# Head attention over all 128 rows, features turned by VectorE, gate logits behind the last expert, and every order written anew

## The chip, the cores and the metric

One Trainium2 chip, and of it one core: TensorE, VectorE (DVE in the rows), ScalarE (ACT), GpSimd (POOL) and SyncE, which issues most transfers. The time of a kernel is its device time in microseconds. Of the kernel before there are three runs.

## What is computed

The input x and the context are 32 batches of 256 tokens with 256 features, all fp32.

```
x = x + tanh(g_xattn) * performer(layernorm(x), ctx, ctx)      # 16 heads of 16, 64 random features, causal
    proj = (q * 256**-0.25) @ random_features                  # [16, 64]; the same for k
    q' = exp(proj_q) + 1e-4;  k' = exp(-|k|^2/2 + proj_k - max over ALL batches of -|k|^2/2) + 1e-4
    out[l] = sum_{j<=l} (q'[l] . k'[j]) v[j] / sum_{j<=l} (q'[l] . k'[j])
x = x + tanh(g_ffn) * ffn(layernorm(x))
    h  = rmsnorm(x);  q = h @ Wq + bq;  k, v = ((h @ Wdown + bdown) @ Wup + bup), per head
    att = softmax(einsum('bthd,btgd->bthg', q, k) / 4)         # over the 16 HEADS of one token
    y2 = x + (einsum('bthg,btgd->bthd', att, v) @ Wo + bo)
    h2 = rmsnorm(y2);  gate = softmax(h2 @ Wg + bg)            # 8 experts
    out = y2 + einsum('btd,edf,bte->btf', h2, We, gate)        # all experts for all tokens
```

## The kernel before

One batch is a matrix of 256 tokens, held as two halves of 128 rows (index t). Exact fp32 products are made out of three rounded ones (`three_passes`): high by high, high by low, low by high, so an operand X has parts `X_hi` (written by ScalarE) and `X_lo` (the rest, by VectorE).

Each batch goes through these stages, named by letters in the signals: q (normalize x, turn x and the context, half norms), r (features: `fk`, `fq`, and their exponentials `ek0..3`, `eq0..3`, to which GpSimd adds 1e-4 in `pk0..3`, `pq0..3`), p (key-query products X00, X01, X10, X11 for the first 128 keys and Y0, Y1 for the second; ScalarE moves X to `att`, VectorE multiplies Y by the causal mask, GpSimd masks the diagonal of X in m00..m11; `av0..av3` multiply by the values, `nt_t` turns the numerators, `den_`, `numerators_over` divide, `attended` adds x), g and f (second normalization, `qq`, `dn`, `kv0`, `kv1`), head attention (scores s, softmax, mix pv), o (output projection, `y2`, second norm, turn of h2), e (gate g and experts `mm00..mm13`, mm1n being the second token half; `gated` adds one expert times its gate to `z`).

Every engine runs a list that was written out by hand for the first batches and then one order, `slot(n)`, repeated for all n: in a slot each stage works on another batch (features on n+2, attention on n+1, head attention on n, output on n-1, experts on n-2 and n-3). There is no planner in the kernel; the order of the calls in `slot` and in the prologue is all that sets it. The eight PSUM banks are dealt out by name in the dictionary `BANK`; two steps with the same bank exclude each other, and the waits `pe.wait_ge(*at(step, batch))` see to it. `if b in (...)` around a wait means that for other batches another wait already covers it.

What the change touches:

- The context and the normalized x are turned by TensorE with the identity, four 128x128 turns each (`keys_turned`, `queries_turned`, L1893), then `k_hi`, `q_hi` are copied from PSUM by ScalarE and `k_low`, `q_low` are taken by VectorE. The half norms h2 are turned by TensorE too (`h_tr_`, L2070).
- Feature products: 4 row groups of 32 rows, 512 columns (`feature_products`, L1915); `norm_products`, L1924, adds the norms with two sets of weights.
- Head attention: q, k and v of a token group are turned by VectorE in 32x32 blocks (`q_turned` L1413, `k_turned` L1441, `v_turned` L1458). ScalarE spreads the queries of the two token halves into `q_bd` with zeros elsewhere (`q_apart`, L854). `head_scores` (L1966) and `head_mix` (L1974) are 128 products each of 32 rows and 32 columns of the array, 16 columns wide, made in four parts of 32 (`PARTS`); `weights_exp` and `ssum_` give the sum of the weights.
- The gate: `gate_products` (L1980, L1982), 8 small products with weights `wg` of 16 columns, in bank g; `gate_bias` adds them up.

Of the kernel before, what the change touches and what calls it, by code (L numbers as in the profile page):

```python
# [5 lines left out]
F32 = mybir.dt.float32  # L6
# [5 lines left out]
P = 128  # L12
# [15 lines left out]
CHUNK_BUFFERS = 8  # L28


BANK = dict(x000=3, x001=7, x010=5, x011=0, y00=6, y01=5, av0=2, x100=6, x101=5, x110=0, x111=1, y10=3, y11=2,
            av1=4, fq0=4, fq1=6, fq2=3, fq3=1, fk0=1, fk1=5, fk2=6, fk3=2, c=5, h=0, x=3, nd0=2, nd1=5, ht=7,
            dn=4, qq=7, kv0=2, kv1=3, s=7, pv=4, otr=0, o=7, h20=2, h21=1, g=2, mm00=0, mm01=0, mm02=4,
            mm03=3, mm10=6, mm11=1, mm12=3, mm13=6)
STAB_BANK = BANK["ht"]
# [45 lines left out]
def build(nc, x_d, ctx_d, gx_d, gf_d, rf_d, g1_d, wq_d, bq_d, wdn_d, bdn_d, wup_d, bup_d,  # L81
          wo_d, bo_d, g2_d, wg_d, bg_d, we_d, out_d):
    ctx = ExitStack()
    with ctx:
# [18 lines left out]
        sel_tok, off_tok = sb("sel_tok", [P, 2]), sb("off_tok", [P, 2])  # L103
        neg_half = sb("neg_half", [P, 4])

        f_hi, f_lo, w_h = sb("f_hi", [P, P], F32R), sb("f_lo", [P, P], F32R), sb("w_h", [P, C, P], F32R)
        sel_h = sb("sel_h", [P, C, 2])
# [5 lines left out]
        wg = sb("wg", [P, C, 2 * E], F32R)  # L113
        we_hi, we_lo = sb("we_hi", [P, C, E * D], F32R), sb("we_lo", [P, C, E * D], F32R)
# [17 lines left out]
        down = sb("down", [P, L], F32R)  # L132
# [8 lines left out]
        q_t, k_t, v_t = sb("q_t", [P, H, 32]), sb("k_t", [P, H, 32]), sb("v_t", [P, HD, 32])  # L141
        q_bd = sb("q_bd", [P, 32, T, H])
        s_max, s_sub, s_exp = sb("s_max", [P, 32]), sb("s_sub", [P, 32, H]), sb("s_exp", [P, 32, H])
        s_sum, s_tok, s_rec = sb("s_sum", [P, 32]), sb("s_tok", [P, T, H]), sb("s_rec", [P, T, H])
        p_bd, p_t = sb("p_bd", [P, 32, T, H]), sb("p_t", [P, 32, 32])

# [4 lines left out]
        o_tok, o_n = sb("o_tok", [P, HD, T, H]), sb("o_n", [P, T, D])  # L151
# [18 lines left out]
        xn = sb("xn", [P, T, D])  # L170
        q_hi, q_lo = sb("q_hi", [P, C, L], F32R), sb("q_lo", [P, C, L], F32R)
        k_hi, k_lo = sb("k_hi", [P, C, L], F32R), sb("k_lo", [P, C, L], F32R)
        h2 = sb("h2", [P, T, 4, 2 * H])
        h_t = sb("h_t", [P, L], F32R)
        v1 = sb("v1", [P, T, H, 32])
        qf, kf = [sb("qf0", [P, PAIRS, L])], [sb("kf0", [P, PAIRS, L])]
# [5 lines left out]
        qf.append(sb("qf1", [P, PAIRS, L]))  # L182
        kf.append(sb("kf1", [P, PAIRS, L]))
# [4 lines left out]

# [5 lines left out]
        gates_in, gammas_in = transfer("gates_in", 1, 2), transfer("gammas_in", 1, 2)  # L194
        wq_in, wo_in, wdn_in, wup_in = transfer("wq_in"), transfer("wo_in"), transfer("wdn_in", 1, 2), transfer("wup_in", 1, 2)
        bdn_in, bqkv_in, bo_in, bg_in = transfer("bdn_in", 1, 2), transfer("bqkv_in", 1, 2), transfer("bo_in"), transfer("bg_in")
        wg_in, we_in, rf_in = transfer("wg_in"), transfer("we_in", 1, 2), transfer("rf_in", 1, 8)

        w_pool = signal("w_pool", "zero_id one_tri ident tri f_scale f_hi f_lo")
        w_act, wa_high, wb_act = signal("w_act", "tanh"), signal("wa_high", "wq wdn wup wo"), signal("wb_act", "wg we0 we1 we2 we3")  # L200
        w_dve = signal("w_dve", "zero_f zero_v1 v1_one half sel_h w_h gamma2")
        wa_dve, wb_dve = signal("wa_dve", "wdn wq wup bkv wo"), signal("wb_dve", "wg we0 we1 we2 we3")
        w_tok = signal("w_tok", "sel_tok off_tok")
        ctx_act, ctx_dve = signal("ctx_act", "square"), signal("ctx_dve", "sum")
        stab_dve, stab_pe = signal("stab_dve", "most min col stab less0 kept less"), signal("stab_pe", "row all")

        batch_signals = [  # L210
            signal("q_pe", "h_tr"),
            signal("q_pe_b", "c_t x_t"),
            signal("q_dve", "h_lo"),
            signal("q_dve_b", "q_st q_mv q_bn k_lo q_lo"),
            signal("q_act", "h_hi"),
            signal("q_act_b", "h_t_"),
            signal("q_act_c", "xn q_hi"),
            signal("q_act_d", "k_hi"),
            signal("q_pool", "rstd q_r"),
            signal("r0_pe", "fk"),  # L220
            signal("r0_pe_b", "fq"),
            signal("r0_act", "ek3"),
            signal("r0_act_b", "ek1"),
            signal("r0_act_c", "ek0"),
            signal("r0_act_d", "ek2"),
            signal("r0_act_e", "eq0"),
            signal("r0_act_f", "eq3"),
            signal("r0_act_g", "eq1"),
            signal("r0_act_h", "eq2"),
            signal("r0_pool", "pq0"),  # L230
            signal("r0_pool_b", "pk0"),
            signal("r0_pool_c", "pk2"),
            signal("r0_pool_d", "pk3"),
            signal("r0_pool_e", "pk1"),
            signal("r0_pool_f", "pq2"),
            signal("r0_pool_g", "pq1"),
            signal("r0_pool_h", "pq3"),
            signal("p0_pe", "X00 X01 Y0 av0 av1"),
# [42 lines left out]
        def at(step, b):  # L281
            return signal_of[step].at(step, b)
# [2321 lines left out]
```

## Time and profile before

| | |
|---|---|
| median of 3 runs | 1260.78 us (1250.12 to 1265.76) |
| the profiled execution, span from its first to its last instruction | 1252.8 us |
| TensorE busy | 1193.6 us, 95% |
| TensorE weight loads (beside the products) | 978.2 us, 78% |
| VectorE busy | 942.0 us, 75% |
| ScalarE busy | 728.5 us, 58% |
| GpSimd busy | 568.1 us, 45% |
| mean granted TensorE clock | 0.988 |

The profile tells of one execution; its span lies 8 us under the median of the runs. Busy time is the union of an engine's instructions, so instructions that overlap count once. In a timeline the second number is the length of a group from its first start to its last end; neighbours overlap, since an instruction's last results are still on their way when the next has started. 40.20 MB are moved in all, 32 GB/s, most of it in the first 30 us, when the whole context is read for the maximum of the half norms.

### The profile page before, as it was taken

What the parts mean: (1) busy time and instruction counts of PE and PEld (TensorE: products, weight loads), DVE (VectorE), ACT (ScalarE), POOL (GpSimd) and SP (SyncE); (2) the same over time, 40 slices, a digit from 0 to 9 for tenths busy, and PEclk for the clock granted to TensorE, in tenths of its full rate; (3) what the DMA queues carried; (4) which work ended last, traced back from release to release, by engine and by line L of the source; (5) the groups of instructions that cost most, each with busy time, mean ns of one, the idle gap of its engine ahead of it and who ended that gap; (6) DMA issues with size and microseconds to landing.
All of it is one profiled execution on the core that took longest, in us unless ns stands there. A gap on an engine that the chain in (4) does not pass through costs nothing.

```text
span 1252.8 us, 55905 instructions
## 1 busy us (share of the span) xinstructions
PE 1193.6 (95%) x25347; PEld 978.2 (78%) x25347; DVE 942.0 (75%) x2206; ACT 728.5 (58%) x1467; POOL 568.1 (45%) x887
## 2 busy tenths in 40 slices
PE   1689899999999999999999999999999999999988
PEld 1467678888888888888888888888788888888876
DVE  7576567787777778777877777777787777777875
ACT  7577545566656556665655665565566656555430
POOL 3455515545444554544445454434545444554320
PEclk9988989999999999999999999999999999999999
DMA  9310000000000000000000000000000000000000
GB/s 304 96 36 20 20 10 29 20 29 28 28 12 28 28 20 28 29 28 11 28 28 20 28 29 28 13 26 29 20 29 28 29 12 28 29 19 11 12 20 17
DMA packets 39005, 40.20 MB, mean 32 GB/s; under 512 B 3440, under 2 KB 38512, under 8 KB 38768
## 3 DMA queue, kind: packets, MB, share of 16 engines
q1 hardware_dynamic: 38384, 36.59, 9.3%
q8 instruction: 199, 3.26, 1.1%
q14 instruction: 38, 0.31, 0.1%
q0 software_dynamic: 384, 0.04, 0.0%
HBM read 28.23 MB, written 8.39 MB: 29 GB/s over the span
## 4 chain that ended last, share of the span: by engine, by line
PE 93%; DVE 2%; DMA 1%; POOL 1%; issue 1%; ACT 1%; SPq 0%; DVEq 0%; POOLq 0%; ACTq 0%
PE ps L1899 14%; PE ps L1901 12%; PE ps L1900 12%; PE ps L1932 10%; PE ps L1947 7%; PE ps L1974 6%; PE ps L1966 6%; PE ps L1940 6%; PE ps L1893 4%; PE ps L1915 4%; PE ps L1957 2%; DMA c_chunk<-in_ctx 1%; PE ps L1982 1%; PE ps L2238 1%; PE ps L2336 1%
## 5 line engine op out<-in xcount | busy, mean ns | idle before, releaser
L1200 DVE SCALAR_TENSOR_TENSOR z<-ps,gate,z 128x256 f32<-128x256 f32 x512 | 245.4, 479 | 80.2 <-PE ps L1901 68.4
L1899 PE MATMUL ps<-we_hi,h_hi 128*128 128x512 f32 x512 | 215.6, 421 | 2.4 <-DVE z L1200 2.4
L1901 PE MATMUL ps<-we_hi,h_lo 128*128 128x512 f32 x512 | 203.9, 398 | 0.0
L1900 PE MATMUL ps<-we_lo,h_hi 128*128 128x512 f32 x512 | 203.7, 398 | 0.0
L1932 PE MATMUL ps<-qf,kf 64*128 64x256 f32 x1024 | 133.5, 401 | 5.1 <-POOL kf L474 2.1
L1899 PEld LDWEIGHTS ps<-we_hi,h_hi 128*128 128x128 f32 x512 | 97.4, 190 | 24.6 <-DVE z L1200 3.3
L453 POOL TENSOR_SCALAR z<-y,tanh_f 128x512 f32<-128x512 f32 x32 | 22.1, 692 | 205.5 <-DVE y L1433 205.3
L1932 PEld LDWEIGHTS ps<-qf,kf 64*128 64x128 f32 x1024 | 97.0, 193 | 23.5 <-issue 7.6
L1901 PEld LDWEIGHTS ps<-we_hi,h_lo 128*128 128x128 f32 x512 | 97.1, 190 | 23.0
L1900 PEld LDWEIGHTS ps<-we_lo,h_hi 128*128 128x128 f32 x512 | 97.5, 190 | 16.0
L1947 PE MATMUL ps<-att,v 128*32 128x256 f32 (+1 forms) x2048 | 98.5, 331 | 2.3 <-issue 1.4
L1966 PEld LDWEIGHTS ps<-k_t,q_bd 32*32 32x32 f32 x8192 | 76.2, 105 | 28.5 <-issue 27.8
L1974 PEld LDWEIGHTS ps<-v_t,p_t 32*32 32x32 f32 x8192 | 75.2, 104 | 21.4 <-issue 20.2
L1966 PE MATMUL ps<-k_t,q_bd 32*32 32x16 f32 x8192 | 83.2, 185 | 5.3 <-issue 5.2
L1947 PEld LDWEIGHTS ps<-att,v 128*32 128x32 f32 x2048 | 57.9, 110 | 36.4 <-issue 11.0
L1974 PE MATMUL ps<-v_t,p_t 32*32 32x16 f32 x8192 | 82.0, 184 | 1.4 <-DVE p_t L1221 0.9
L1940 PE MATMUL ps<-qf,kf 64*128 64x128 f32 x1024 | 76.8, 289 | 3.0 <-issue 1.5
L854 ACT ACTIVATE q_bd<-q_t,sel_tok 128x512 f32<-128x512 f32 x64 | 77.2, 1266 | 2.5 <-DVE q_t L1413 2.4
L1940 PEld LDWEIGHTS ps<-qf,kf 64*128 64x128 f32 x1024 | 64.8, 192 | 6.7 <-ACT att L713 2.5
L744 ACT ACTIVATE nt<-ps 128x512 f32<-128x512 f32 x32 | 19.1, 597 | 86.8 <-PE ps L1947 86.8
L525 POOL TENSOR_TENSOR y<-y,b_o 128x512 f32<-128x512 f32 x32 | 41.3, 1290 | 53.4 <-ACT y L917 53.4
L898 ACT ACTIVATE h_hi<-ps 128x256 fp32r<-128x256 f32 x32 | 12.4, 386 | 86.1 <-PE ps L2336 86.1
(217 smaller groups left out, 3056.1 us busy)
## 6 DMA issues: line engine op xcount, KB each, us to landing
c_in<-in_ctx SPq DMA_DIRECT2D x32, 256.0 KB, 4.0
x_in<-in_x SPq DMA_DIRECT2D x32, 256.0 KB, 2.8
out<-z SPq DMA_DIRECT2D x32, 256.0 KB, 2.2
c_chunk<-in_ctx SPq DMA_DIRECT2D x14, 512.0 KB, 8.8
stage<-in_L_ffn_We SPq DMA_DIRECT2D x2, 1024.0 KB, 9.3
c_chunk<-in_ctx SPq DMA_DIRECT2D x2, 256.0 KB, 8.2
stage_q<-in_L_ffn_Wq SPq DMA_DIRECT2D x1, 256.0 KB, 8.5
stage_u<-in_L_ffn_Wup SPq DMA_DIRECT2D x2, 128.0 KB, 6.5
```

The lines of the kernel that those rows point to most:

```text
L854: last = act.activation(q_bd[:, :, t, :], q_t[:, :, :].rearrange("p h n -> p n h"), ACT.Copy, scale=sel_tok[:, t:t + 1])
L1200: return dve.scalar_tensor_tensor(out=z[e % 2][:, t, :], in0=ps[:, bank, ex % 2 * D:(ex % 2 + 1) * D], scalar=gate[:, t, ex:ex + 1], in1=z ...
L1893: last = pe.transpose(out[:, c * L + t * P:c * L + (t + 1) * P], src[:, t, c * P:(c + 1) * P], ident[:, :])
L1899: pe.matmul(out, a_hi(c), b_hi(c), start=(c == 0), stop=False)
L1900: pe.matmul(out, a_hi(c), b_lo(c), start=False, stop=False)
L1901: last = pe.matmul(out, a_lo(c), b_hi(c), start=False, stop=(c == C - 1))
L1915: last = pe.matmul(ps[:, BANK[f"f{of}{r}"], :], weight[own, :], src[own, :, :].rearrange("p c l -> p (c l)"), start=(n == 0), stop=(n == 2 ...
L1932: last = pe.matmul(ps[:, banks[half], j * L:(j + 1) * L], kf[b % 2][r, pr, 0:P], qf[b % 2][r, pr, :], start=True, stop=True)
L1940: last = pe.matmul(ps[:, banks[half], j * P:(j + 1) * P], kf[b % 2][r, pr, P:L], qf[b % 2][r, pr, P:L], start=True, stop=True)
L1947: last = pe.matmul(ps[32 * j:32 * j + 32, bank, half * L + part * P:half * L + L], v1[:, part, 8 * oct + 2 * j + half, :], att[:, half, j, ...
L1966: last = pe.matmul(ps[r, BANK["s"], n * H:(n + 1) * H], q_bd[r, n, :, :], k_t[r, :, n], start=True, stop=True, tile_position=(32 * j, 32 * j))
L1974: last = pe.matmul(ps[r, BANK["pv"], n:512:32], p_t[r, n, :], v_t[r, :, n], start=True, stop=True, tile_position=(32 * j, 32 * j))
```

## The change

No result changes in kind. What is done otherwise:

- `keys_turned`, `queries_turned`, `h_tr_` leave TensorE. VectorE turns the context, xn and the norms in 32x32 blocks inside SBUF (`c_t_`, `x_t_`, `h_tr_`, into `c_raw`, `x_raw`, `h_raw`). The features of a block then come out block by block: `tokens_of` picks them. `k_lo`, `q_lo` are GpSimd's. One set of norm weights is enough.
- `qf` and `kf` have one buffer each.
- Scores: the keys are spread by ScalarE into `k_bd` (four copies, each zero outside its 32 rows), and a product takes all 128 rows: 32 output rows, 64 columns. The mix: GpSimd spreads the values into `v_bd` with a column of ones (four scalings, 4 x 17 = 68 columns), so the sum of the weights comes out of the product; `weights_exp` and `ssum_` go. `q_t`, `k_t`, `v_t` are stored with the token outside and the head inside. For the values the down rows are copied in another order of tokens, `down_v`, by GpSimd.
- The gate weights are columns 2048 to 2055 of `we_hi`, `we_lo`; the last expert is a product of its own of 264 columns (`mm0g`, `mm1g`), the seventh one of 256.
- `BANK`, all orders and nearly all waits are new, and TensorE's list has no prologue of its own: after the stabilizer it is `slot(n)` from n = 3 on. On TensorE the slot is: mm1g, av2, pv, av3, mm10, fq, kv1, mm00, o_tr, kv0, mm11, o, nt_t, mm12, mm01, X01, X00, Y0, mm02, mm03, mm13, h2_t1, h2_t0, hn_t, av0, s, av1, X11, Y1, X10, qq, dn, mm0g, fkp, fk.

```diff
-            def head_scores(part):
-                for n in range(32 * part // PARTS, 32 * (part + 1) // PARTS):
-                    for j in range(4):
-                        r = slice(32 * j, 32 * j + 32)
-                        last = pe.matmul(ps[r, BANK["s"], n * H:(n + 1) * H], q_bd[r, n, :, :], k_t[r, :, n],
-                                         start=True, stop=True, tile_position=(32 * j, 32 * j))
+            def head_scores(bank):
+                for n in range(32):
+                    c, m = n % 4, n // 4
+                    last = pe.matmul(ps[32 * c:32 * c + 32, bank, :].rearrange("p (a m g) -> p m a g", a=4, m=8)[:, m],
+                                     q_bd[:, n, :, :].rearrange("p t h -> p (t h)"), k_bd[:, n, :, :],
+                                     start=True, stop=True, tile_position=(0, 32 * c))
+            def head_mix(banks):
+                width = 4 * (HD + 1)
+                for n in range(32):
+                    a, m = n % 4, n // 4
+                    last = pe.matmul(ps[32 * a:32 * a + 32, banks[m // 4], m % 4 * width:(m % 4 + 1) * width],
+                                     p_t[:, 8 * a + m, :], v_bd[:, 8 * a + m, :, :].rearrange("p c d -> p (c d)"),
+                                     start=True, stop=True, tile_position=(0, 32 * a))
+            def pv_(b):
+                if b + 1 < NB:
+                    pe.wait_ge(*at("d_lo", b + 1))
+                if b + 3 < NB:
+                    pe.wait_ge(*at("ek2", b + 3))
...
+            def mm00_(b):
+                if b + 4 < NB:
+                    pe.wait_ge(*at("eq0", b + 4))
...
+            def h2_t1_(b):
+                if b:
+                    pe.wait_ge(*at("a02", b - 1))
...
+            def mm1g_(b):
...
+                expert_products(b, 1, slice(7 * D, E * D + E), BANK["mm1g"]).then_inc(*up("mm1g", b))
+            def c_t_(b):
...
+                dve.wait_ge(*c_load.at(b))
+                dve.transpose(blocks(c_raw), c_in[b % 2][:, :, :].rearrange("p t (a d) -> p (t a) d", d=32)).then_inc(*up("c_t", b))
+            def x_t_(b):
+                dve.wait_ge(*at("xn", b))
+                dve.transpose(blocks(x_raw), xn[:, :, :].rearrange("p t (a d) -> p (t a) d", d=32)).then_inc(*up("x_t", b))
+            def h_tr_(b):
...
+                dve.transpose(blocks(h_raw), h2e[:, :, :, :].rearrange("p t a k -> p (t a) k")).then_inc(*up("h_tr", b))
-                dve.transpose(q_t[:, :, :], qkv[:, :, 0:D].rearrange("p t (h d) -> p h t d", d=HD)).then_inc(*up("q_t", f))
+                dve.transpose(q_t[:, :, :].rearrange("p n h -> p h n"), qkv[:, :, 0:D].rearrange("p t (h d) -> p h t d", d=HD)).then_inc(*up("q_t", b))
+            def k_lo_(b):
+                pool.wait_ge(*at("k_hi", b))
+                pool.tensor_tensor(k_lo[:, :], c_raw[:, :], k_hi[:, :].bitcast(F32), ALU.subtract).then_inc(*up("k_lo", b))
+            def v_bd_(b):
+                pool.wait_ge(*at("v_t", b))
+                for a in range(4):
+                    last = pool.tensor_scalar(v_bd[:, :, a, 0:HD], v_t[:, :, :], sel_blk[:, a:a + 1], 1.0, ALU.mult, ALU.mult)
+            def k_bd_(b):
...
+                for a in range(4):
+                    act.activation(k_bd[:, :, a, :], k_t[:, :, :], ACT.Copy, scale=sel_blk[:, a:a + 1])
-                    last = act.activation(q_bd[:, :, t, :], q_t[:, :, :].rearrange("p h n -> p n h"), ACT.Copy, scale=sel_tok[:, t:t + 1])
+                    act.activation(q_bd[:, :, t, :], q_t[:, :, :], ACT.Copy, scale=sel_tok[:, t:t + 1])
```

ScalarE's order in a slot: hn, h_t, h2_hi1, h2_hi0, ht_hi, nt0, x111, x110, x101, k_hi, xn, x100, p_bd, q_hi, d_hi, ek1, ek2, ek0, ek3, gexp, nt1, eq0, eq2, ot_hi, eq1, h_hi, q_bd, eq3, y, sq, k_bd, x010, x000, h2n, x001, x011. VectorE's: y2, h_lo, den, o_x, a12, g_bn, a01, y00, y01, a02, a03, a13, v_t, h2_lo0, h2_lo1, ht_lo, smax, q_bn, c_t, ssub, y10, y11, bqq, x_t, p_t, d_lo, ga, gm, gate, o_tok, s_rec, a1g, a0g, q_t, h_tr, a10, bkv1, a00, ot_lo, bkv0, k_t, a11. GpSimd's: d_v, pk2, pk3, o_n, pk0, pq0 to pq3, z0, x1, r2, g_r, v1, m00, m01, yb, v_bd, q_r, k_lo, m10, m11, q_lo, pk1.

## Rows read from the trace of the kernel before

**Rows 1.** The page: busy time by engine, then the span in 40 slices.
```profile
PE 1193.6 (95%) x25347; PEld 978.2 (78%) x25347; DVE 942.0 (75%) x2206; ACT 728.5 (58%) x1467; POOL 568.1 (45%) x887
...
PE   1689899999999999999999999999999999999988
...
PEclk9988989999999999999999999999999999999999
```

**Rows 2.** Window from gate to gate: PE, PEld, DVE, ACT, POOL busy, clock, DMA.
```profile
235.60:1148.30 912.70, 910.77 (x19803) 753.52 (x19802) 708.95 (x1676) 549.88 (x1124) 435.13 (x676) 1.00 0.08 24
```

**Rows 3.** Timeline of TensorE, one batch: start, length in us, instruction, count.
```profile
600.37 0.17 PE L1980 MATMUL ps<-wg,h_hi 128*128 128x16 f32 x1
...
601.25 2.00 PE L1932 MATMUL ps<-qf,kf 64*128 64x256 f32 x16
603.18 1.27 PE L1974 MATMUL ps<-v_t,p_t 32*32 32x16 f32 x128
604.38 1.16 PE L1940 MATMUL ps<-qf,kf 64*128 64x128 f32 x16
605.47 0.44 PE L2070 MATMUL ps<-ident,h 128*128 128x128 f32 x2
605.67 0.48 PE L1899 MATMUL ps<-we_hi,h_hi 128*128 128x512 f32 x1
...
607.67 1.51 PE L1947 MATMUL ps<-att,v 128*32 128x256 f32 x32
609.11 2.00 PE L1932 MATMUL ps<-qf,kf 64*128 64x256 f32 x16
...
614.85 0.60 PE L1893 MATMUL ps<-ident,c_in 128*128 128x128 f32 x4
615.29 0.60 PE L1893 MATMUL ps<-ident,o_n 128*128 128x128 f32 x4
...
616.88 0.28 PE L1899 MATMUL ps<-wq_hi,ht_hi 128*128 128x256 f32 x1
617.00 0.28 PE L1900 MATMUL ps<-wq_lo,ht_hi 128*128 128x256 f32 x1
...
626.68 1.27 PE L1966 MATMUL ps<-k_t,q_bd 32*32 32x16 f32 x128
627.88 0.50 PE L1899 MATMUL ps<-we_hi,h_hi 128*128 128x512 f32 x1
628.22 0.40 PE L1900 MATMUL ps<-we_lo,h_hi 128*128 128x512 f32 x1
628.45 0.40 PE L1901 MATMUL ps<-we_hi,h_lo 128*128 128x512 f32 x1
```

**Rows 4.** Weight loads grouped by form: busy us, mean ns, idle before.
```profile
L1947 PEld LDWEIGHTS ps<-att,v 128*32 128x32 f32 x2048 | 57.9, 110 | 36.4 <-issue 11.0
```

**Rows 5.** VectorE grouped by form: busy us, mean ns, idle before.
```profile
L1200 DVE SCALAR_TENSOR_TENSOR z<-ps,gate,z 128x256 f32<-128x256 f32 x512 | 245.4, 479 | 80.2 <-PE ps L1901 68.4
...
L1215 DVE TENSOR_SCALAR var_f<-mvg 128x2 f32<-128x2 f32 x32 | 33.6, 1051 | 1.1
...
L1413 DVE STREAM_TRANSPOSE q_t<-qkv 128x512 f32<-128x512 f32 x32 | 22.4, 701 | 0.1
...
L1646 DVE COPY b_qkv<-stage_b 128x256 f32<-128x256 f32 x2 | 1.0, 545 | 0.0
```

**Rows 6.** ScalarE grouped by form.
```profile
L854 ACT ACTIVATE q_bd<-q_t,sel_tok 128x512 f32<-128x512 f32 x64 | 77.2, 1266 | 2.5 <-DVE q_t L1413 2.4
L911 ACT ACTIVATE p_bd<-s_sub,off_tok 128x512 f32<-128x512 f32 x64 | 42.8, 716 | 13.2 <-DVE s_sub L1509 13.2
```

**Rows 7.** GpSimd grouped by form.
```profile
L487 POOL TENSOR_TENSOR x<-o_x,x_in 128x512 f32<-128x512 f32 x32 | 41.9, 1310 | 3.6 <-DVE o_x L1480 1.3
```

**Rows 8.** Timeline of ScalarE, two neighbours.
```profile
603.79 0.59 ACT L719 ACTIVATE att<-ps 128x512 f32<-128x512 f32 x1
604.27 0.60 ACT L725 ACTIVATE att<-ps 128x512 f32<-128x512 f32 x1
```

More of the change, by code:

```diff
@@ L279, in build @@
-        signal_of = {step: s for s in batch_signals for step in s.steps}
-        def at(step, b):
+        gammas_in, wq_in, wo_in = transfer("gammas_in", 1, 4), transfer("wq_in"), transfer("wo_in", 1, 2)
+        down_in = transfer("down_in", 1, 6)
+        bqkv_in, wg_in = transfer("bqkv_in", 1, 2), transfer("wg_in", 1, 2)
+        we_in, rf_in = transfer("we_in", 1, 2), transfer("rf_in", 1, 8)
+        signals = [
+            signal("once_pe0", "most_turned stab_all"),
+            signal("pe0", "fk fq X01 X00 Y0 av1 X11 Y1 X10"),
+            signal("pe1", "av3 nt_t hn_t qq dn"),
+            signal("pe2", "kv1 kv0 s pv"),
+            signal("pe3", "o_tr o h2_t1 h2_t0 mm1g mm10 mm00"),
+            signal("pe4", "mm11 mm12 mm01 mm02 mm03 mm13"),
+            signal("once_dve0", "sel_h v1_one least_ least stabilizer less0 kept less wq_lo wdn_lo"),
+            signal("keys_dve0", "key_sums"),
+            signal("dve0", "h_lo h_tr"),
+            signal("dve1", "q_st q_mv q_bn x_t"),
+            signal("dve2", "c_t"),
+            signal("dve3", "y00 y10 den_s den_d den o_x g_st g_mv g_bn"),
+            signal("dve4", "y01 y11"),
+            signal("dve5", "ht_lo bqq d_lo bkv0 k_t"),
+            signal("dve6", "q_t v_t smax ssub"),
+            signal("dve7", "p_t o_tok s_rec ot_lo y2 h2_lo0"),
+            signal("dve8", "h2_lo1 ga gmax gm gsum grec gate a1g a10_ a10 a00_ a11_ a11 a12_ a12 a01_ a01 a02_ a02 a03 a13"),
+            signal("dve9", "a0g"),
+            signal("keys_act0", "square"),
+            signal("act0", "h_hi"),
+            signal("act1", "h_t ek1 eq0"),
+            signal("act2", "k_hi xn q_hi"),
+            signal("act3", "ek2 ek3 eq2 x010 nt0 x111 x101"),
+            signal("act4", "ek0 eq1 x000 x100"),
+            signal("act5", "eq3 x001 nt1"),
+            signal("act6", "x011"),
+            signal("act7", "hn ht_hi d_hi"),
+            signal("act8", "y p_bd ot_hi"),
+            signal("act9", "sq h2n h2_hi1 gexp"),
+            signal("act10", "h2_hi0"),
+            signal("once_pool0", "zero_id f_scale f_hi tri"),
+            signal("pool0", "rstd q_r q_lo pq3"),
+            signal("pool1", "k_lo v1"),
+            signal("pool2", "m00 m01 m10 m11 x1 r_f g_r"),
+            signal("pool3", "d_v v_bd"),
+            signal("pool4", "o_n z_y z0 ms_e r2"),
+        ]
@@ L365, in _ @@
+            for n in range(3, NB + 7):
                 slot(n)
@@ L1187, in _ @@
+            for n in range(3, NB + 7):
                 slot(n)
```

3324 lines of the change are left out of this document (1463 added, 1861 removed).

## The prediction

> **What bounds the kernel now.** I read the page first: the matmul row is busy 95% of the span, its slices are at nine tenths from the sixth to the last but two, and the granted clock from the seventh on [rows 1]. Then the stretch between the gate product of batch 3 and that of batch 28, 25 repeats of one written-out order: TensorE 910.8 of 912.7 us, VectorE 709, ScalarE 550, GpSimd 435 [rows 2]. So one batch costs 36.5 us, all of it TensorE; per batch VectorE has 28.4 us, ScalarE 22.0, GpSimd 17.4. Last, TensorE's own order over one batch, from the gate product at 600.37 on [rows 3]. The durations there overlap, so a price is the distance between two starts. Any saving on TensorE is a saving of time until another engine, or a loop of waits through several, comes up to it.
>
> **TensorE, part by part.** (1) Turning the context, the normalized x and the half norms leaves TensorE. Four turns take 0.44 us (614.85 to 615.29), twice, and the two of the norms 0.20 (605.47 to 605.67) [rows 3]: 1.05 us less per batch, 32x512-wide feature products staying as they are.
> (2) The eight gate products, 600.37 to 601.25, take 0.88 us [rows 3]. Their eight columns now ride on the eighth expert, and that pair is cut into a 256- and a 264-column product. A 256-column product costs 0.12 (616.88 to 617.00), a 512-column one 0.23 (628.22 to 628.45) [rows 3], so the six extra instructions of each token half cost about 0.01 each: 0.8 us saved.
> (3) Head scores and head mix. Now each is two runs of 128 instructions of 32x32 tiles and 16 columns; a run takes 1.20 us (603.18 to 604.38, and 626.68 to 627.88) [rows 3], so 4.8 us per batch. After the change each is 64 instructions with all 128 rows, 32 output rows, and 64 or 68 columns, four side by side. The nearest row is the attention product with tiles of 128x32: 32 instructions, half of 256 and half of 128 columns, in 1.44 us (607.67 to 609.11) [rows 3], thus eight groups of four at 0.18. The 64-row products give the slope: pairs of 256 columns at 1.93/8 = 0.241 (601.25 to 603.18), of 128 at 1.09/8 = 0.136 (604.38 to 605.47) [rows 3], that is 0.82 ns a column and at most 31 ns fixed, part of which is paid once a run. A group of four at 64 columns then lies between 0.056 and 0.085 us; 32 groups give 1.8 to 2.7 us. The bound from above is a group that waits a whole weight load, 110 ns [rows 4]: 3.5. I take 2.0, near the low end, because the attention groups leave under 10 ns beside their columns: 2.8 us saved, between 1.3 and 3.0.
> (4) Each change of tile shape costs: the first expert product after one takes 0.34 (627.88 to 628.22) against 0.23 [rows 3]. The old order changes shape 17 times a batch, the new one 11 times (scores and mix now stand between attention products of the same shape, and the key products stand together): 6 x 0.11 = 0.65 saved.
> Sum 5.3 us: TensorE's work falls from 36.5 to 31.2 us per batch. The value products cut in two cost nothing (four of 256 for two of 512).
>
> **The other engines.** VectorE loses k_lo and q_lo, the sum of the weights and its turn (about 0.6 + 0.6 + 0.6 + 0.25) and gains three turns of 512 elements at 0.61 (0.70 less the 0.09 by which neighbours overlap) [rows 5]: no change, 28.4. ScalarE: q_bd read its input at a step of 128 bytes and took 1266 ns, twice, where p_bd, with the same output, takes 716 [rows 6]; with q_t turned the other way it saves 1.1. Four k_bd of 512 elements add 2.5, the exponentials for the sum leave (0.5): about 23 us. GpSimd gets k_lo and q_lo (1.31 each by the x1 row [rows 7]), four scalings for v_bd (as 512-element work at 0.65) and the copy of the down rows (0.5): 17.4 + 5.7 = 23, and its idle joints of 0.08 make it 26. All stay under 31.2, but not by much, and VectorE carries the greatest unknown: the three turns of queries, keys and values now store at a step of 64 bytes. The row that shows such a store is the bias copy: 1.0 us for two halves of 256 elements, of which one stores at that step [rows 5]; split evenly it is 0.5 each. From below the turns cost nothing more; from above, if that half took 0.7 of the 1.0, some 0.7 us each, 2.1 per batch. I take 0.4 each, 1.2 per batch: VectorE near 29.6. The Trainium skill (SBUF — State Buffer, "Door 1: The DMA port swizzle") says that each access that crosses to a new 16-byte line pays; the q_bd row agrees for reads, no row shows it for a turn's store, and by that rule alone the sum would lean to the upper end.
> One thing may come back: var_f takes 1051 ns for two elements a row [rows 5]; it looks blocked by a GpSimd operation. In the new order it may lose the 0.9 us or keep it; with GpSimd fuller, other small operations may be caught. Zero taken, 0.9 either way.
>
> **New waits.** Queries and keys have one buffer now, not two, and the banks are dealt anew, so most TensorE steps wait. Three are near the path. (a) The mix stands behind ek2 (its bank): from the end of X10 ScalarE has x101, k_hi, xn, x100, p_bd, q_hi, down, ek1, ek2 to do, eight starts 0.48 apart [rows 8], 1.25 for p_bd [rows 6], 0.37 for the down rows, and 0.3 for hand-over and tail: 5.8; TensorE needs qq, down, gate part, features, mm1g and av2, about 5.4: 0.4 us late, with av3 and mm10 queued behind. (b) mm00 waits for eq0, which waits for fq, with only kv1 (0.5) between against a hand-over and 0.6: 0.3 late. (c) h2_t1 waits for a02 on VectorE, which comes after its norms and four other adds: 0 to 0.6 late. Together 0.7 to 1.3; in an order as dense as this I take the upper end: 32.5 us per batch.
> The whole loop through the engines is the check: X10, then ScalarE as in (a) with ek0 and ek3 (6.8), VectorE from the gate to y2 (eight 512-element steps at 0.61, eight gated adds of 479 ns less 30 [rows 5], small ones 1.0: 9.5), ScalarE from y to hn with the four k_bd (8.1), TensorE from the turn of hn to X10 (5.6), hand-overs 0.3: 30.3, or 31.1 with two slow stores. It is under 32.5, but has no room for one more.
>
> **The time.** The 25 repeats save 25 x 4.0 = 100 us. The ends (some seven batches' work in 340 us) are half waiting, the stabilizer still comes after all context chunks, and fq(0) now stands behind two exponentials: of 7 x 5.3 = 37 I take 20, between 0 and 37. Total 120: the profiled span would go from 1252.8 to 1133. The median of the runs is 1260.8, 8 us above that span; taken off it, the forecast is 1141 us. 2% of the median, 25 us, is about what a measurement here can tell from no change: 1235.6 to 1286.
>
> **The rivals.**
> Forecast, TensorE bound with small stalls, 31.9 to 33.6 per batch: 1110 to 1175. Chance 0.54.
> Full gain: the waits fall within slack and 31.1 holds: 25 x 5.4 + 30 = 165, so 1096. For it: the old order ran with 2 us of 913 idle. Against: (a) and (b). 0.14.
> The loop through VectorE and ScalarE becomes the bound: stores at 0.7 in q_t, k_t, or var_f and a neighbour blocked, take 30.3 to 34 or 36. At 35: 25 x 1.5 + 10 = 47, so 1213; it lies from 1175 to 1236. 0.20.
> No change: the same loop at 36 to 37, 1236 to 1286. 0.05.
> Slower: four products that share all 128 rows do not run side by side when they are short, and each instruction waits for its weight load. Place: head_scores and head_mix, 128 instructions a batch. It decides from (5.3 + 2.0)/128 = 57 ns an instruction, against 16 in my sum; at the 110 ns of a load [rows 4] they cost 14 us, the batch 31.2 + 12.1 = 43.3, the time 1260.8 + 25 x 6.8 + 7 x 3 = 1452. Against it: 45 ns an instruction in the attention rows, with as many loads. 0.07.
> The Trainium skill (TensorE: Matmul & The Clock Gate, Part 3, "The mechanism") has a rule for that rival: a load overlaps running products only when its row group differs, and here it never differs. The attention rows have the same shape and contradict it.
> That the turns don't do what they say can be excluded from the text: turning within 32x32 blocks is matched by features taken per block.
>
> **Range and chances.** 1095 to 1205 leaves out 0.07 below and about 0.13 above. Faster by over 2%: 0.54 + 0.14 + 0.20 = 0.88; within: 0.05; slower: 0.07.
>
> **What would show it.** The distance between two gate-carrying products near the middle is 32.5 us; TensorE's idle 1 to 2 us of it, before pv (ended by ScalarE's kf), mm00 (by qf) and h2_t1 (by z). Scores and mix take 0.9 to 1.3 us a run. q_bd falls to about 0.7. If q_t, k_t and v_t show over 1.2 us, or TensorE idles over 3 us a batch, the third case holds; if scores take over 3 us, the last. Wrong would be a steady distance under 31 or above 34.

## The result, and the profile after

The changed kernel takes 1119.3 us (median of 4 runs, 1117.6 to 1121.8) against 1259.8 for the kernel before beside it: ratio 0.890, 95% interval 0.885 to 0.894. The forecast was 1141 with a range of 1095 to 1205, and "faster". The profiled span fell from 1252.8 to 1117.9 us. The page of the kernel after, busy time, the slices and the head of the chain of waits:

```profile
span 1117.9 us, 31579 instructions
PE 1034.7 (93%) x12867; PEld 841.2 (75%) x12867; DVE 938.5 (84%) x2173; ACT 757.0 (68%) x1563; POOL 756.8 (68%) x1111
...
PE   0576899999999999999999999999999999999988
...
PEclk9988899999999999999999999999999999999999
...
PE 52%; DVE 24%; DMA 7%; ACT 7%; POOL 6%; issue 2%; SPq 1%; POOLq 0%; DVEq 0%; ACTq 0%
```

Beside [rows 1]: half the instructions of TensorE are gone (25347 to 12867), VectorE's share rose from 75% to 84% with 3.5 us less work, GpSimd's from 45% to 68% with 189 us more. The chain still has TensorE first, but with only 52% of the span where the page before gave it 93%, and two names in it are new to watch: VectorE, and the loads (DMA). Now 25 repeats of the new order, between the first turned numerator of batch 5 and that of batch 30 (columns as in [rows 2]):

```profile
217.90:1021.60 803.70, 795.37 (x10053) 649.92 (x10052) 698.47 (x1649) 573.52 (x1200) 581.65 (x850) 1.00 0.09 26
```

So the distance per batch is 803.7/25 = 32.15 us against 36.51, and 25 x 4.36 = 109 of the 134.9 us that the span lost. The ends gave the other 26. VectorE has 27.9 us of work a batch, ScalarE 22.9, GpSimd 23.3. TensorE's timeline at the places that the prediction priced:

```profile
614.04 0.86 PE L1903 MATMUL ps<-att,v 128*32 128x256 f32 x16
614.71 1.08 PE L1928 MATMUL ps<-k_bd,q_bd 128*32 128x64 f32 x64
615.61 0.40 PE L1903 MATMUL ps<-att,v 128*32 128x256 f32 x4
...
623.03 0.51 PE L1872 MATMUL ps<-k_hi,f_hi 32*128 32x512 f32 x4 [0.71 <-DVE qkv L1316]
...
625.90 1.15 PE L1937 MATMUL ps<-v_bd,p_t 128*32 128x68 f32 x64
626.85 0.43 PE L1903 MATMUL ps<-att,v 128*32 128x256 f32 x4
...
630.60 0.28 PE L1922 MATMUL ps<-wup_lo,down_v 128*128 128x256 f32 x1
630.91 0.50 PE L1857 MATMUL ps<-we_hi,h_hi 128*128 128x512 f32 x1
```

Read by distances of starts: the head scores take 0.90 us (614.71 to 615.61) and the mix 0.95 (625.90 to 626.85), where [rows 3] had four runs of 1.20. Attention products stand on both sides of them with the same tiles, and no start is lost. One fp32 product is two instructions in the trace: `head_scores` makes 32 products, and its row counts 64, so the prediction's group of four instructions is two products. At 623.03 TensorE has waited 0.71 us for VectorE's addition of the query bias (L1316, step bqq). The last value product and the first expert product of mm00 are 0.31 apart instead of 0.12. The waits over the same 25 batches, first those of TensorE's weight loads, then VectorE's (name waited for, us in total, times, longest):

```profile
PEld ps L1857 <- issue: 22.4, 75, 0.4
...
PEld ps L1872 <- DVE qkv L1316: 9.1, 14, 0.9
PEld ps L1857 <- ACT qf L730: 5.9, 25, 0.2
PEld ps L1903 <- DVE z L1142: 4.2, 25, 0.2
PEld ps L1937 <- DVE down L1332: 4.1, 17, 0.3
```

```profile
DVE bn L1276 <- DMA x_in<-in_x: 28.5, 25, 2.1
DVE bn6g L1198 <- POOL x L424: 24.2, 25, 1.1
DVE p_t L1327 <- ACT p_bd L683: 14.8, 25, 0.9
...
DVE c_raw L1290 <- DMA c_in<-in_ctx: 6.5, 7, 1.4
```

The rows with "issue" name no one that is waited for; the four large ones (this one and three of 9 to 14 us) come alike in every batch. Of the named waits none is above 0.4 us a batch for TensorE. VectorE, though, waits 1.14 us a batch for the load of x and 0.26 for that of the context. The operations that answer to [rows 5 to 7], from groups by line over the same window:

```profile
L1426 DVE STREAM_TRANSPOSE k_t<-qkv 128x512 f32<-128x512 f32 x26 | 28.7, 1103 | 0.9
L1385 DVE STREAM_TRANSPOSE q_t<-qkv 128x512 f32<-128x512 f32 x25 | 26.8, 1071 | 0.0
L1249 DVE STREAM_TRANSPOSE v_t<-qkv 128x512 f32<-128x512 f32 x25 | 26.5, 1060 | 0.0
...
L1356 DVE SCALAR_TENSOR_TENSOR gate<-gx,tanh_f,gr 128x16 f32<-128x16 f32 x25 | 15.2, 606 | 0.9
L1205 DVE TENSOR_SCALAR var_f<-mvg 128x2 f32<-128x2 f32 x25 | 4.2, 170 | 0.9
```

```profile
L762 ACT ACTIVATE q_bd<-q_t,sel_tok 128x512 f32<-128x512 f32 x52 | 34.7, 722 | 0.0
```

The turns with a store at a step of 64 bytes take 1.06 to 1.10 us where they took 0.70, var_f fell from 1051 to 170 ns, and q_bd from 1266 to 722.

### The profile page after: what moved, and what is told of

It reads as the page before. It is cut to its first block, busy times and chain, and to the rows that moved or that the text cites. A ratio compares the mean times of both kernels' runs of the same rounds, so it can differ in the third digit from the quotient of the medians.

```text
span 1117.9 us, 31579 instructions
## 1 busy us (share of the span) xinstructions
PE 1034.7 (93%) x12867; PEld 841.2 (75%) x12867; DVE 938.5 (84%) x2173; ACT 757.0 (68%) x1563; POOL 756.8 (68%) x1111
## 4 chain that ended last, share of the span: by engine, by line
PE 52%; DVE 24%; DMA 7%; ACT 7%; POOL 6%; issue 2%; SPq 1%; POOLq 0%; DVEq 0%; ACTq 0%
PE ps L1857 10%; PE ps L1858 7%; PE ps L1859 7%; DVE z L1142 6%; PE ps L1888 6%; PE ps L1903 5%; PE ps L1872 4%; DMA c_in<-in_ctx 4%; DMA x_in<-in_x 3%; PE ps L1937 3%; PE ps L1896 3%; POOL x L424 2%; POOL z L417 2%; DVE k_t L1426 2%; PE ps L1851 2%
## 5 line engine op out<-in xcount | busy, mean ns | idle before, releaser
L1857 PE MATMUL ps<-we_hi,h_hi 128*128 128x512 f32 (+2 forms) x640 | 238.8, 373 | 5.8 <-DVE s_sub L1296 1.7
L1858 PE MATMUL ps<-we_lo,h_hi 128*128 128x512 f32 (+2 forms) x640 | 223.7, 350 | 0.0
L1859 PE MATMUL ps<-we_hi,h_lo 128*128 128x512 f32 (+2 forms) x640 | 223.7, 349 | 0.0
L1859 PEld LDWEIGHTS ps<-we_hi,h_lo 128*128 128x128 f32 x640 | 120.2, 188 | 17.2
L1858 PEld LDWEIGHTS ps<-we_lo,h_hi 128*128 128x128 f32 x640 | 120.5, 188 | 11.6
L475 POOL TENSOR_SCALAR v_bd<-v_t,sel_blk 128x512 f32<-128x512 f32 x128 | 88.3, 710 | 13.2 <-DVE v_t L1249 13.2
L789 ACT ACTIVATE k_bd<-k_t,sel_blk 128x512 f32<-128x512 f32 x128 | 81.5, 708 | 4.6 <-DVE k_t L1426 4.6
L773 ACT ACTIVATE y<-x,shift_f,r_f 128x256 f32<-128x256 f32 x64 | 35.0, 594 | 49.5 <-DVE y L1155 49.5
L507 POOL TENSOR_TENSOR q_lo<-x_raw,q_hi 128x512 fp32r<-128x512 f32 x32 | 41.2, 1288 | 30.4 <-ACT q_hi L689 30.4
L380 POOL TENSOR_TENSOR o_n<-o_tok,s_rec 128x512 f32<-128x512 f32 x32 | 41.6, 1301 | 22.2 <-DVE s_rec L1367 21.8
```

What stands on the lines that cost most here:

```text
L380: pool.tensor_tensor(o_n[:, :, :].rearrange("p t (h d) -> p d t h", d=HD), o_tok[:, 0:HD, :, :], s_rec[:, :, :].unsqueeze(1).to_broadcast( ...
L475: last = pool.tensor_scalar(v_bd[:, :, a, 0:HD], v_t[:, :, :], sel_blk[:, a:a + 1], 1.0, ALU.mult, ALU.mult)
L507: pool.tensor_tensor(q_lo[:, :], x_raw[:, :], q_hi[:, :].bitcast(F32), ALU.subtract).then_inc(*up("q_lo", b))
L789: act.activation(k_bd[:, :, a, :], k_t[:, :, :], ACT.Copy, scale=sel_blk[:, a:a + 1])
L1857: pe.matmul(out, a_hi(c), b_hi(c), start=(c == 0), stop=False)
L1858: pe.matmul(out, a_hi(c), b_lo(c), start=False, stop=False)
```

## The experiments

All comparisons use the medians of the runs; a distance is that between the turned numerators of batch 5 and batch 30, divided by 25. Every diff is against the changed kernel unless it says otherwise.

**Column tiles in another order.** The slower rival said that short products on all 128 rows would not run side by side. To see what makes them do so, only their order was changed:

```diff
-                for n in range(32):
-                    c, m = n % 4, n // 4
+                for c, m in [(c, m) for c in range(4) for m in range(8)]:
+                    n = 4 * m + c
```

(and the same in head_mix).

> The changed kernel with the head scores and the head mix in another order: all eight products of one column tile, then the next, instead of the four column tiles in turn. Same products, same results. Theory A (four neighbours on different column tiles run side by side although they share all 128 rows, so a group of four at 64 columns takes 0.056 us): with neighbours on the same tile each instruction pays at least its 64 columns, 27 ns at 0.42 ns a column, so a run of 64 takes at least 1.7 us against 0.90 in the profile after; two runs a batch then add 1.6 us or more, 32 batches 50 us or more, so at least 1165; if each instruction also waits for its weight load (110 ns), a run takes 7 us and the time is about 1119 + 32 x 12 = 1500. Theory B (short products run at 14 ns each whatever the tile): 1119, runs of 0.90.

Measured: 1243.0 us (ratio to before 0.988, 0.985 to 0.991). TensorE's timeline, scores and mix, and the window:

```profile
569.71 2.99 PE L1928 MATMUL ps<-k_bd,q_bd 128*32 128x64 f32 x61
572.49 0.42 PE L1903 MATMUL ps<-att,v 128*32 128x256 f32 x3
572.54 0.33 PE L1928 MATMUL ps<-k_bd,q_bd 128*32 128x64 f32 x3
...
582.15 3.15 PE L1936 MATMUL ps<-v_bd,p_t 128*32 128x68 f32 x61
585.08 0.42 PE L1903 MATMUL ps<-att,v 128*32 128x256 f32 x3
```

```profile
233.77:1134.12 900.35, 898.53 (x10052) 754.94 (x10051) 704.64 (x1649) 571.32 (x1200) 580.91 (x850) 1.00 0.08 24
```

The first 61 instructions of a run take 2.78 and 2.93 us (the last three start among the attention products), 47 ns each instead of 14, and the distance is 36.01. Theory A holds, its lower form: the instruction costs more than its 27 ns of columns, but not a whole weight load of 110. With eight products in a row on one column tile, the same 128 instructions make a batch 3.87 us longer; of the 4.36 that the change gained, nearly all hangs on the inner loop's order.

**The old tiles in the new kernel.** Scores and mix as 32x32 tiles with 16 and 17 columns:

```diff
+                    for j in range(4):
+                        r = slice(32 * j, 32 * j + 32)
+                        last = pe.matmul(ps[r, bank, n * H:(n + 1) * H], q_bd[r, n, :, :]...,
+                                         k_bd[r, n, j, :], start=True, stop=True, tile_position=(32 * j, 32 * j))
```

> The changed kernel with head scores and head mix as the old tiles: 128 products of 32x32 with 16 (17) columns each, on the new data; the heads' results are then wrong, all other work stays. Theory A (TensorE's own work sets the time after the change as before it, and this part was 4.88 us a batch before and 1.84 after by the distances of starts): +3.0 us a batch plus four changes of tile shape at 0.1, so 3.4 x 32 = 109, less up to 0.6 a batch of stalls that vanish: 1210 to 1230. Theory B (a loop through VectorE and ScalarE sets the time and TensorE has slack): 1119 to 1150.

Measured: 1524.0 us (ratio to before 1.214, 1.207 to 1.221). Neither theory: the price was to be 100 us and was 405. The distance is 45.3 us, and the gaps between neighbouring instructions inside the runs show why. In six batches from 500 us on, the 12 runs of 256 hold 15 gaps of 0.8 to 3.6 us, 37 us together, and the waits put them down to "issue", that is to nothing that the profile shows. The window has a mean granted clock of 0.87, between the full 2.4 GHz and the lower level of 1.2, where every other window here has 0.96 or more:

```profile
260.22:1393.37 1133.15, 985.02 (x19653) 786.97 (x19651) 711.47 (x1649) 571.23 (x1200) 580.04 (x850) 0.87 0.07 20
```

45.3 less 6.2 of gaps is 39.1, and at 0.87 of full clock that is 34 to 39 us of work; the 35.6 that was expected lies in it, but this is a bound, not a price. To separate the gaps from the clock, the scores alone got their old tiles, in two runs of 128 that stand apart, as the kernel before had them:

```diff
+                head_scores(BANK["s"], 0)                               # ahead of av1
...
                 X11_(n - 3)
+                s_more_(n - 5)                                            # head_scores(BANK["s"], 1)
                 Y1_(n - 3)
```

> The changed kernel with only the head scores as old 32x32 tiles, in two runs of 128 instructions apart from each other as before the change (the heads' results are then wrong). Theory A (TensorE bound; in e2_small_tiles the surplus over its 3.4 us a batch came from TensorE's queue running dry in runs of 256 instructions at 9 ns): 2.40 for 0.90 and three more changes of tile shape, +1.7 to 1.9 a batch, 1119 + 31 x 1.8 = 1175, between 1165 and 1185, and no gap over 0.5 us within a run. Theory B (the queue runs dry in short runs too): gaps of 2 us and more in the runs, 1220 or more. Theory C (TensorE has slack): under 1140.

Measured: 1272.2 us (ratio to before 1.012, 1.008 to 1.016). TensorE's timeline over one pair of runs:

```profile
585.94 1.26 PE L1929 MATMUL ps<-k_bd,q_bd 32*32 32x16 f32 x128
...
588.98 0.48 PE L1929 MATMUL ps<-k_bd,q_bd 32*32 32x16 f32 x35
591.35 0.96 PE L1929 MATMUL ps<-k_bd,q_bd 32*32 32x16 f32 x93 [1.89 <-issue]
```

An undisturbed run takes 1.19 us, as before. But from 400 to 1000 us, 16.2 batches, there are 28 gaps of 0.7 to 2.1 us, 37 us together. The second run of each batch has one; four are in first runs, the other seven in the short products beside them. So theory B is right that short runs have gaps too, and the effect is real in both kernels: TensorE stands still between two instructions of one run, waiting for no semaphore.

The price itself can still be read. The distance is 37.0 at a mean granted clock of 0.96, but in 11 of the 25 batches the clock is 1.00 throughout. They take 35.75 us on average, of which gaps over 0.6 us are 2.0, so 33.7 is left (33.5 to 33.9 in each). Six of the eleven stand in a row, 35.7 us each:

```profile
574.62:789.09 214.47, 204.24 (x3566) 164.99 (x3565) 167.79 (x398) 137.59 (x288) 140.11 (x205) 1.00 0.08 24
```

33.7 is 1.6 above the base's 32.15, and 2.0 above those batches of the base in which nothing waits (31.7). Theory A expected 1.7 to 1.9: its price for the old scores holds. The rest of the 37.0 is 2.2 of gaps and 1.1 of clock.

**What TensorE waits for in the gaps.** Not for the data that move: gaps come while the input loads are under way and also when no packet moves at all. Their place tells more. Numbered in the order of their starts, with weight loads, products and waits together, TensorE's instructions have 67 gaps over 0.6 us in the 25 batches of the kernel with both parts in old tiles, 42 in this one and 2 in the kernel before (four runs of 128 a batch; 98 of 100 runs without a gap over 0.3 us). All of them lie whole multiples of 256 instructions apart, within one. The only other gap of that size, one in each of the two kernels with old tiles, is a wait with a name. The page has a queue with packets of 16384 bytes, here that of the first kernel:

```profile
q8 instruction: 198, 3.24, 0.9%
```

There are 150 such packets in this kernel, 199 in the kernel before and 102 in the changed one; TensorE's instructions divided by 256 are 198.7, 150.7, 199.4 and 102.7. Each of the 111 gaps ends 1.2 to 1.6 us after one of these packets has landed, and two of the packets never start less than 3.2 us apart, while 256 instructions of an old run (128 loads and their products, 9.4 ns a pair) are used up in 1.2 us. So TensorE waits for its own program, which comes in blocks of 256 instructions. Place and time of every gap show it; no experiment changed it. The changed kernel, with runs of 64 at 14 ns, has no gap over 0.3 us in its 50 runs.

**Gate logits on their own.** Behind each cut pair, four products of 8 columns:

```diff
-                expert_products(b, 1, slice(7 * D, E * D + E), BANK["mm1g"]).then_inc(...)
+                expert_products(b, 1, slice(7 * D, E * D), BANK["mm1g"])
+                gate_products(b, 1, BANK["mm1g"]).then_inc(*up("mm1g", b))
```

> The changed kernel with the gate logits as products of their own of 8 columns, four for each token half, right behind the eighth expert, whose pair stays cut in two; the pass with the low part of the gate weights is left out, so that there are eight products as before. Theory A (each costs what an instruction costs, 0.11 us, as before): +0.85 a batch, 27 us, less what stalls give back: 1138 to 1146. Theory B (short products fit in the shadow of the long ones): within 3 us of 1119.

Measured: 1130.1 us (ratio 0.899, 0.895 to 0.903), 8 below the lower end. In the trace the eight take 0.96 us a batch by their starts, as theory A has it, but the distance rose from 32.15 to 32.45 only. The two expert pieces that they follow, up to the next instruction of another kind, grew by 0.32 us each where nothing waits, 0.63 a batch. The waits say where the other half of that went:

```profile
PEld ps L1872 <- DVE qkv L1316: 2.3, 6, 0.5
```

Against 9.1 us and 14 times above: four of the eight stand right ahead of the key features and fill part of the stall there (0.16 a batch). The other four stand ahead of av2 and the mix, and the mix's wait for the down rows, 4.1 us above, is gone (0.15). So TensorE's price of a step is not its price in time while the stall exists.

**Contiguous stores.** The turned queries, keys and values stored without a step:

```diff
-  dve.transpose(q_t[:, :, :].rearrange("p n h -> p h n"), ...
+  dve.transpose(q_t[:, :, :].rearrange("p n h -> p (n h)").rearrange("p (h n) -> p h n", n=32), ...
```

> The changed kernel with the turned queries, keys and values stored contiguously instead of at a step of 64 bytes (the heads' results are then wrong). Both theories: the three VectorE instructions fall from 1.06-1.10 to about 0.70 us. Theory A (TensorE bound, VectorE has slack): the time stays within 5 us of 1119, and VectorE waits longer. Theory B (VectorE sets the distance): 1.1 us a batch goes, 1085.

Measured: 1112.3 us (ratio 0.884, 0.882 to 0.887); the distance is 31.99. Groups by line:

```profile
L1426 DVE STREAM_TRANSPOSE k_t<-qkv 128x512 f32<-128x512 f32 x26 | 18.5, 711 | 0.9
...
```

The other two take 702 and 701 ns. The step of the store costs 0.36 to 0.39 us each, 1.1 a batch, and of it 0.16 comes back as time. Theory B falls; theory A is off by 2 us, because VectorE isn't free: it is a little late at one place. The next runs name it.

**Where the stall comes from.** In SP's queue a slot stores batch n - 3, and only then loads x and the context; the store waits for the last gated add. Three kernels, with the changed one again as base.

> The changed kernel once more, as the base for the three kernels beside it: 1119 within 3 us by every theory.

Measured: 1117.6 us (1115.1 to 1124.0).

The loads ahead of the store:

```diff
-                store_(n - 3)
                 load_x_(n + 2)
                 load_c_(n + 2)
+                store_(n - 3)
...
-                if b == 3:
+                if b >= 3:
                     sp.wait_ge(*at("v1", b - 2))
+                    sp.wait_ge(*at("c_t", b - 2))
```

> The changed kernel with the two input loads ahead of the store in each slot of SP's queue. In the profile after, the load of x leaves only once the store's wait on the last gated add is over, and VectorE then waits 1.1 us a batch for x and 0.2 for the context, which puts the query bias and with it the key features (who wait for that bias to free their bank) late. Theory A (the stall of 0.4 us a batch ahead of the key features comes from the queue order of the loads): VectorE's waits on loads go, TensorE's distance falls from 32.15 to its undisturbed 31.7, 25 to 30 batches, so 1105 to 1112. Theory B (something else comes just as late there, the low part of the keys on GpSimd, which ends only 0.4 us sooner): VectorE's waits go or move, time within 3 us of the base.

Measured: 1108.8 us (1108.4 to 1109.9), ratio to before 0.881 (0.879 to 0.884). SP's issues, first in the kernel after, then here:

```profile
613.90 0.38 SPq L272 DMA_DIRECT2D out<-z  x1
614.33 0.47 SPq L278 DMA_DIRECT2D x_in<-in_x  x1
614.84 0.50 SPq L284 DMA_DIRECT2D c_in<-in_ctx  x1
```

```profile
603.11 0.37 SPq L278 DMA_DIRECT2D x_in<-in_x  x1
603.57 0.41 SPq L285 DMA_DIRECT2D c_in<-in_ctx  x1
608.38 0.38 SPq L272 DMA_DIRECT2D out<-z  x1
```

The load of x used to leave 5.7 us after its buffer came free (GpSimd's x1 ends at 608.6), behind the store; now it leaves as the buffer comes free. Window, and all of VectorE's waits for more than 0.4 us a batch:

```profile
216.20:1010.77 794.57, 792.76 (x10052) 649.80 (x10051) 698.03 (x1649) 571.03 (x1200) 581.82 (x850) 1.00 0.09 27
```

```profile
DVE bn6g L1199 <- POOL x L425: 24.3, 25, 1.1
DVE p_t L1328 <- ACT p_bd L684: 22.9, 25, 0.9
DVE qkv L1317 <- PE ps L1860: 19.5, 25, 0.8
```

The waits for loads are gone, the bias now waits for TensorE instead of the other way round, and the distance is 31.78 and, but for the first of the 25, the same within 0.1 from batch to batch. Theory A holds. This kernel is the fastest of the study, 8.8 us (0.8%) under the base.

The query bias one step sooner, with the loads late:

```diff
                 y10_(n + 3)
-                y11_(n + 3)
                 bqq_(n + 2)
+                y11_(n + 3)
```

> The changed kernel with the query bias ahead of the last masked product on VectorE, one 0.6 us step sooner; the loads stay late. Theory A (the bias is what the key features wait for): its stall of about 0.4 us a batch shrinks by 0.2 to 0.4, 1109 to 1115. Theory B (the low part of the keys follows right behind, as the loads are as late as before): less than 3 us from the base.

Measured: 1119.4 us, no gain. Theory B, in that other things are as late: TensorE's waits for the bias fell from 9.1 to 2.6 us, but waits for the low part of the keys (three), for kf and for the down rows ahead of pv came in their place; the last grew from 4.1 to 6.8 us. The cause is what makes VectorE late, not which step stands first.

More work on VectorE, two further turns of 1.07 us (one in v_t, one at the head of q_bn), loads late, and then loads early:

```diff
+                for out in (spare, v_t):
+                    last = dve.transpose(out..., qkv[:, :, 2 * D:3 * D]...)
...
+                if b >= 5:
+                    dve.transpose(spare..., qkv[:, :, 2 * D:3 * D]...)
```

> The changed kernel with two more turns of the values into a spare tile on VectorE, 1.07 us each, about 2.0 a batch, both ahead of its wait for x. Theory A (TensorE sets the distance; VectorE has 4 us of idle time, of which 1.3 waits for the loads at this place): 1.3 us is swallowed by the load wait, the rest delays the query bias and so the key features by 0.6 at most: 1119 + 25 x 0.6 = 1134, between 1125 and 1140. Theory B (no coupling at all): within 5 us of 1119. Theory C (VectorE is as good as the bound, my third case): 2.0 a batch comes out in full, 1170 or more.

> The kernel with the loads first (1108.8), and the same 2.0 us a batch of extra turns on VectorE that cost 8 to 10 us with the loads late. Theory A (that cost came by way of the query bias, which the late loads hold back; with the loads early VectorE has 0.8 us of slack there and over 3 us in all): 0.4 to 1.2 of the 2.0 us shows up as a stall ahead of the key features at most, 1109 to 1125. Theory B (VectorE's own sum, 30 of 32 us, bounds it): 1150 or more.

Measured: 1127.2 and 1123.4 us, both inside theory A's ranges. Their windows, and TensorE's largest named wait in each:

```profile
219.21:1026.92 807.71, 798.23 (x10052) 653.80 (x10051) 739.07 (x1699) 575.77 (x1200) 581.80 (x850) 1.00 0.09 26
```

```profile
PEld ps L1878 <- DVE qkv L1322: 11.4, 25, 0.9
```

```profile
217.91:1023.49 805.58, 798.16 (x10053) 653.63 (x10051) 737.03 (x1699) 576.26 (x1200) 583.13 (x850) 1.00 0.08 26
```

```profile
PEld ps L1879 <- DVE qkv L1323: 9.1, 25, 0.4
```

With the loads late, 1.6 us more VectorE work a batch (739.07 less 698.47, over 25) costs 0.16 in distance, since 1.4 of it goes into the wait for the loads (28.5 + 6.5 us before, 1.3 now). With the loads early it costs 0.44, because that slack is no longer there. Both end near 32.2 to 32.3: at 29.5 us of VectorE work a batch the key features wait in all 25 batches. At 27.9, where the changed kernel is, they wait in 14.

**The low parts back on VectorE.** k_lo and q_lo as before the change, k_lo ahead of the bias, q_lo behind p_t (signals and both orders edited accordingly).

> The changed kernel with the low parts of keys and queries back on VectorE, as before the change: 0.6 us each on VectorE in place of 1.3 each on GpSimd; the one of the keys stands ahead of the query bias. Theory A (time goes only through the key features' wait): the bias comes 0.5 to 0.6 us later, so 0.5 a batch, 1119 + 14 = 1133, between 1126 and 1138. Theory B (GpSimd was the late one): unchanged or faster, 1112 to 1121. Small VectorE operations that GpSimd had held up (gates 524 ns, difference of gate logits 306) should come back toward 244 and 192 if GpSimd's two long subtractions were what held them.

Measured: 1135.3 us (ratio 0.904, 0.901 to 0.907), distance 32.61: theory A. TensorE waits 18.1 us for the bias in the 25 batches. Moving the two to GpSimd is thus worth 16 us, though VectorE had idle time. The gates did not get faster (681 ns between 400 and 1000 us, against 584 there in the changed kernel), so these two subtractions are not what slows them.

**One more wait.** On top of the loads first, the turn of the head output ahead of mm00:

```diff
+                o_tr_(n - 6)
                 mm00_(n - 7)
-                o_tr_(n - 6)
```

> The kernel with the loads first (1108.8), and on TensorE the turn of the normalized head output ahead of the first expert pair of the first token half, so that this pair, which waits 0.2 us a batch for the first query feature to be read out of its bank, has 0.43 us of other work before it. Theory A (the distance of 31.73 is TensorE's work plus that one stall): 31.5 a batch, 1109 - 25 x 0.2 = 1104, between 1101 and 1107. Theory B (the turn itself now waits for GpSimd's scaling, which ends 0.3 us before): within 2 us of 1109.

Measured: 1113.6 us (1112.5 to 1118.7): 5 slower than without. The wait of mm00 is gone, but the distance fell by 0.05 only (31.73). A wait of X01 for o_x took its place in part (3.8 us in 25 batches, 10 times), and the ends lost some 6 us. That 0.2 us wait was not to be had this way.

## Why the prediction came out as it did

The forecast case held: TensorE bound, small stalls, 31.9 to 33.6 us a batch; measured 32.15. The total is 22 us under the figure: 9 by 0.35 us a batch, 6 by the ends, which saved 26 us and not 20, and 7 by the offset: the span was taken off a median that stood 8 us above it, while the new median is 1.4 above its span.

TensorE's sum, by distances of starts over the 25 repeats:

| step of the prediction | forecast, us | measured, us |
|---|---|---|
| (1) turns of context, x, norms | -1.05 | -1.0 |
| (2) gate logits | -0.8 | about -0.6 |
| (3) scores and mix | -2.8 (1.3 to 3.0) | -3.04 (4.88 to 1.84) |
| (4) fewer changes of tile shape | -0.65 | about -0.4 |
| value products cut in two | 0 | 0.1 |
| stalls | +0.7 to +1.3 | about +0.6 |
| distance | 32.5 | 32.15 |

The distance came out as near as this partly by luck: (3) saved 0.24 more than the sum had, (2) and (4) 0.45 less, and 1.3 were added for stalls of which 0.6 came, more than half of it at a place that I had not named. The 0.6 is the two largest named waits, 0.36 and 0.24; the products themselves stand idle for 0.33 us a batch (8.33/25).

**Term (3)** was the largest and sat just beyond its upper bound: a group of four instructions at 64 columns takes 0.056 us (0.90/16), the low end of the slope from [rows 3]. The fixed part of a run does not show here, where the runs on either side have the same tiles. Undoing the scores alone cost 1.6 to 2.0 us a batch at full clock and without the gaps, in line with the starts in the two profiles (2.46 against 0.89 for the scores) and the changes of shape that come with the old tiles. **The slower rival** had the right place and a wrong condition. The Trainium skill (TensorE: Matmul & The Clock Gate, Part 3, "The mechanism") ties the overlap of weight load and products to differing row groups; here the row group never differs, and an instruction takes 14 ns with the column tiles in turn and 47 with eight products in a row on one tile. The measurement decides: it is enough that neighbouring products have different column tiles. My threshold of 57 ns would not have been reached even so; the serial kernel, at 47, is still 1.2% faster than before, less than the 2% that I called a change.

**Terms (2) and (4)** were a little too large. The first product of a run still pays about 0.1 us after each change of shape, and the two pieces of the eighth expert start one run more; the value products now follow the query features, and their first pays it too (630.14 to 630.37 in the trace).

**The new waits** failed as named, and their sum was half of the 1.3 that I took. Of my three, (b), mm00 behind eq0, is there in every batch, 0.24 us of a weight load's wait (5.9/25). (a), pv behind ek2, is not: where pv waits, it waits for the down rows, 0.16. (c), h2_t1 behind a02, never shows. What I did not name is the largest, the key features behind the query bias of two batches before (9.1/25 = 0.36). Nor did I name av0 behind the gated add a03, 0.17 in every batch (4.2/25). I priced ScalarE's order to the tenth and left out the queue that feeds VectorE: a load behind a store that waits for the last gated add. The taking up of a buffer had been followed to x1, but not to the place of the load in SP's order, and that is worth 9 us, shown by the kernel that swaps them.

**VectorE.** The store at a step of 64 bytes costs 0.36 to 0.39, as taken (0.4), and the contiguous kernel shows that the step alone does it. The Trainium skill's rule of 16-byte lines (SBUF — State Buffer, "Door 1: The DMA port swizzle") has the right sign, but "the upper end" of 0.7 was not reached. VectorE's sum came to 27.9 against 29.6, of which 0.9 is var_f, the gain I had put at zero; I did not trace the other 0.8. ScalarE (22.9 against 23) and GpSimd (23.3 against 23) were right, q_bd too (0.72 against 0.7).

**The third case**, the loop through VectorE, I gave 0.20 at up to 35 us a batch. The runs with 1.6 us more on VectorE put it in its place: the loop is felt at 0.2 to 0.5 us a batch from where the kernel is, and each further us there costs a part of itself. The long wait of 1.3 us that the loads caused was also what swallowed it.

## What to carry to other kernels

Small products on all 128 rows are cheap only if neighbours write different column tiles: put the column tile in the inner loop, 14 against 47 ns an instruction here. Count instructions too: a run of the old tiles uses up 256 of them in 1.2 us, no trace here brings in two blocks of 256 less than 3.2 us apart, and the two kernels that put old tiles into the new order paid 2 and 6 us a batch for that. When a program written out by hand is reordered, follow each load to its place in its own queue; a store that waits ahead of it delays it by that wait, and the bill comes two engines later. And an engine with 13% idle time is not free: what counts is how late it is at the one step that the bound engine waits for.

## What was not expected of the hardware

- TensorE ran out of its own program: gaps of 0.6 to 3.9 us inside runs of short products, always whole multiples of 256 instructions apart, each over 1.2 to 1.6 us after a 16384-byte packet of the queue `instruction` had landed. Weight loads count like products. The kernel before, with its four runs of 128 farther apart, had two such gaps in 25 batches.
- A small VectorE operation can take as long as a GpSimd operation beside it. The timelines of VectorE and GpSimd in the kernel after:

```profile
627.32 0.69 DVE L1356 SCALAR_TENSOR_TENSOR gate<-gx,tanh_f,gr 128x16 f32<-128x16 f32 x1
```

```profile
627.37 0.62 POOL L370 TENSOR_SCALAR kf<-kf 128x512 f32<-128x512 f32 x1
```

  Both end within 0.02 us. The gate took about 0.25 before the change, and var_f went the other way, from 1.05 to 0.17. That they end together is seen; that one holds up the other was not tested by itself.
